# A tensor product pass over sorted edges: its dense part takes 468 destinations instead of 136

## The chip, the cores and the metric

The kernel is one program on one core of a Trainium2 chip. Its inputs lie in the chip's memory, and the metric is the device time in microseconds of one launch. The core's engines are TensorE (PE in the profile, its weight loads apart as PEld), VectorE (DVE), ScalarE (ACT), GpSimd (POOL) and SyncE (SP), which here only issues transfers.

## The reference

Four graph layers run one after the other on 6,250 nodes of 128 channels and 200,000 edges; `dst` is sorted and strongly skewed (node 0 has thousands of edges, node 6,000 about sixteen). The change touches the second layer alone, a tensor product that is linear in the source node's channels `x1` and in the nine numbers `x2` of each edge:

```
for k, (i1, i2, io) in enumerate(_INSTR):
    seg = einsum('uvw,ijk,eui,evj->ewk', weights[k], W3J[k], x1s, x2s) * NORM[k]
    out = out.at[:, e:f].add(seg)
...
agg = segment_sum(out, dst)
```

So a destination's result is the sum over nine components c of a fixed 128x128 matrix `w_mix[c]` times the sum over its edges of x2[c] times h[src], where h are the normalised node features.

## The kernel before

The program is a row of stages with a barrier between them. The stage here is `tensor_pass`, from about 1007 to 2711 us of the span. It has two parts that share the engines.

**The gathered part.** Edges are taken in groups of 1,024 (8 tiles of 128), four groups (u = 0 to 3) to a round. For each group GpSimd gathers the 1,024 rows of h by source with 8 indirect transfers (L3007), into one of four buffers, which it may overwrite once the same u of the round before is summed. VectorE makes one-hots of the destinations in a range of 16 and multiplies them by the nine edge numbers (`hoty`, L3092). TensorE does the group in four slots q = 0 to 3, each with two tiles: `sums` (L3217, 4 instructions of 144 columns; every f32 matmul is two instructions in the trace), then a share of `mix` for the group before (L3232, 18 instructions of 128 columns over a group), in slot 1 also `place_sums` (L3244), and last what the plan of the dense part puts into the slot. ScalarE copies each slot's sums out of PSUM (`take_parts`, L3039) and, at a group's end, the mixed result (`take_mixed`, L3049), for which TensorE's first `mix` of the next group waits, since both use the bank `pm`. VectorE adds the placed result to the accumulator (L3111).

**The dense part** serves the first destinations, those with the most edges, without gathering (class `Dense`). Each destination has a fixed number of visits, each a matmul of 128 edges: a one-hot of the source's low 7 bits against nine edge numbers spread over 49 blocks (L3255, 441 columns), so that a destination's visits sum its weights over all source nodes. After a destination's last visit ScalarE copies the 441 columns into `d_sums` (L3023). After a batch of destinations 49 matmuls multiply h by `d_sums` (`apply_batch`, L3264), ScalarE copies (L3029), nine matmuls mix (`mix_batch`, L3272), and VectorE adds (`add_nodes`). SyncE loads the edges of each destination (L2950, L2951), `prepare` turns them into numbers and masks, and `hots_of_nodes` makes the one-hots for TensorE, a group ahead. `Dense.plan` lays all pieces over the slots. The edges of the first SKIP rounds belong wholly to dense destinations, and the gathered part leaves those rounds out.

SyncE also issues the gathered part's index loads (L2962), each behind the dense loads that stand ahead of it in the program.

Of the kernel before, what the change touches and what calls it, by code (L numbers as in the profile page):

```python
# [27 lines left out]
P = 128  # L28
# [1139 lines left out]
class Dense:  # L1168


    NODES, BATCH, SKIP = 136, 17, 7
    RUN, RING, SLICES, FIRST, TAIL = 2, 6, 7, 32, 12

    def __init__(self, nc, ctx, sh):
# [6 lines left out]
        for b in range(self.batches):  # L1181
            mine = range(b * self.BATCH, (b + 1) * self.BATCH)
            if sum(self.caps[i] for i in mine) % self.RUN:
                self.caps[next(i for i in mine if not i or self.caps[i] < self.caps[i - 1])] += 1
# [5 lines left out]
        assert self.NODES <= 2 * P and self.NODES % self.BATCH == 0 and self.RUN == 2  # L1190
# [8 lines left out]
        self.windows = sb("dense_windows", [1, 1], I32)  # L1199
        self.plan()  # L1200
# [7 lines left out]
    def size(self, b):  # L1208
        return self.first[(b + 1) * self.BATCH] - self.first[b * self.BATCH]

    def room(self):

        return self.size(0) + self.size(1)

    def place_of(self, v):

        b = next(b for b in range(self.batches) if v < self.columns(b).stop)
        return v - self.columns(b).start + b % 2 * self.size(0)

    def places(self, b):  # L1220
        at = self.place_of(self.columns(b).start)
        return slice(at, at + self.size(b))

    def plan(self):


        pieces, gaps = [], 0
        for b in range(self.batches):
            for i in range(b * self.BATCH, (b + 1) * self.BATCH):
                for v in range(self.first[i], self.first[i + 1]):  # L1230
                    pieces.append(("visit", i, v))
            pieces.append(None)
            for k in range(self.SLICES):
                pieces.append(("apply", b, k))
            pieces.append(None)
            pieces.append(("mix", b, 0))
            pieces += [None, None]
# [4 lines left out]
        assert len(pieces) <= room  # L1242
        self.at = [[] for _ in range(slots)]
        for n, piece in enumerate(pieces):
            if piece is not None:
                self.at[self.FIRST + n * room // len(pieces)].append(piece)
        self.hots_at = [[] for _ in range(self.groups)]
        self.prep_at = [[] for _ in range(self.groups)]
        self.adds_at = [[] for _ in range(self.groups)]
        for slot, here in enumerate(self.at):  # L1250
            for kind, n, k in here:
                group = slot // self.parts
                if kind == "visit" and k % self.RUN == 0:
                    self.hots_at[group - 1].append(k)
                    for b in range(self.batches):
                        if k <= self.columns(b).start < k + self.RUN:
                            self.prep_at[group - 2].append(b)
                if kind == "mix":
                    self.adds_at[group].append(n)
        self.loads_at = [[] for _ in range(self.groups)]  # L1260
        for b in range(self.batches):
            after = 0
            if b >= 2:
                after = 4 + next(g for g, here in enumerate(self.hots_at) if self.columns(b - 2).stop - self.RUN in here)
            for n in range(self.BATCH):
                while len(self.loads_at[after]) == 6:
                    after += 1
                self.loads_at[after].append(b * self.BATCH + n)

    def done_before(self, slot):  # L1270

        return self.at[slot - 1] if slot else []


def dense_stage(nc, core, dense):
# [3 lines left out]
    with ExitStack() as ctx:  # L1279
# [16 lines left out]
        p_row = ctx.enter_context(nc.psum_tensor("p_row_dense", [P, 512], F32))  # L1296
        p_all = ctx.enter_context(nc.psum_tensor("p_all_dense", [P, 512], F32))
# [13 lines left out]
        def _(pe):  # L1311
            for c in range(2):
# [3 lines left out]
            nc.tensor.matmul(p_all[:, 0:N + 2], ones[0:1, 0:P], row[:, :], start=True, stop=True).then_inc(row_spread, 1)  # L1316
# [1501 lines left out]
def tensor_pass(nc, core, dense, w_mix, src, src_tiles, attr, attr_laid, table):  # L2818
# [5 lines left out]
    with ExitStack() as ctx:  # L2824
# [13 lines left out]
        PAIRS = J // 2  # L2838
        tiles = U * J
        assert R % 2 == 0  # L2840
        V, B, N, RUN, RING = dense.visits, dense.BATCH, dense.NODES, dense.RUN, dense.RING
        seen, skipped_tiles = dense.seen_tiles, dense.SKIP * U * J
        A = sh.blocks
        wide = Y * A
        assert wide <= 512 and Y * B <= 512
# [12 lines left out]
        moved = sb("moved", [P, 6])  # L2858
# [7 lines left out]
        edge_no = sb("edge_no", [P, seen])  # L2866
        done_far = sb("done_far", [P, seen])
        d_src = sb("d_src", [P, dense.room()], I32)
        d_part = sb("d_part", [P, dense.room()], I32)
        d_lo = sb("d_lo", [P, dense.room()])  # L2870
        d_hi = sb("d_hi", [P, dense.room()])
        d_attr = sb("d_attr", [P, dense.room(), Y])
        d_mask = sb("d_mask", [P, dense.room()])
        d_steps = sb("d_steps", [P, dense.most + 1])
        d_hot = sb("d_hot", [P, RING, P])
        d_row = sb("d_row", [P, RING, Y, A])
        d_sums = sb("d_sums", [P, A, Y, B])
        d_agg = sb("d_agg", [P, Y * B])
        ps = [bank(f"ps{i}") for i in range(4)]
        pm = bank("pm")  # L2880
        p_hot = bank("p_hot")
        hot = p_hot[:, 0:2 * J * RANGE].rearrange("p (s j d) -> p s j d", s=2, d=RANGE)
        steps = p_hot[:, 256:256 + P]
        d_high = p_hot[:, 384:384 + RUN * A].rearrange("p (v a) -> p v a", a=A)
        pw = bank("pw")[:, 0:WIN]
        pd = bank("pd")
# [11 lines left out]
        part_taken = sems("part_taken", 4)  # L2898
# [1801 lines left out]
```

## Time and profile before

| what | value |
|---|---|
| time, median of 3 runs (lowest to highest) | 7041.6 us (7026.89 to 7049.93) |
| span of the profiled execution | 5516.4 us |
| the profiled execution's own time | not among the times; median less span is 1525.2 us |
| busy over the whole span: PE, DVE, ACT, POOL | 76%, 51%, 42%, 69% |
| tensor pass: first gather to the last add | 1015.4 to 2708.3 us |

The span is from the first to the last instruction of the trace; what lies around it has no row. The shares over the whole span are means over stages with different limits, so the rows below are taken from the pass alone.

### The profile page before, as it was taken

How to read it: one execution, taken by the hardware profiler on the slowest of the kernel's cores; microseconds unless marked ns; L12 is line 12 of the kernel's file. 1: busy time of each engine (PE TensorE's matmuls, PEld its weight loads, DVE VectorE, ACT ScalarE, POOL GpSimd, SP SyncE). 2: the span in 40 equal slices, each digit the busy share in tenths (PEclk: the TensorE clock that was granted, in tenths of full speed). 3: DMA queues.
4: the chain of work that ended last, by engine and by line, in shares of the span. 5: the costliest groups of instructions: out<-in, count | busy, mean ns of one | idle time of the engine just before them, and what ended most of it. 6: DMA issues, size and time to landing. Idle time of an engine off the chain costs nothing. (4 is left out here: it accounts for less than half of the span.)

```text
span 5516.4 us, 98683 instructions
## 1 busy us (share of the span) xinstructions
PE 4206.6 (76%) x27638; PEld 3117.4 (57%) x27833; DVE 2829.6 (51%) x8882; ACT 2333.7 (42%) x5698; POOL 3823.3 (69%) x3904
## 2 busy tenths in 40 slices
PE   3399997477777787777757777778777878579985
PEld 2167665355656666656645555555555555446664
DVE  7898665444444444344365555555555555542225
ACT  2545554222222222222366666666666666331003
POOL 0267776677777777777467777777777777477774
PEclk7599998699999999999878888888888888689997
DMA  1134444222222222222233333333333333165552
GB/s 59 43 134 152 165 155 140 69 58 57 59 58 58 60 58 59 58 59 57 53 76 86 78 86 78 82 82 78 86 78 86 78 85 80 40 215 179 173 173 61
DMA packets 357101, 495.36 MB, mean 90 GB/s; under 512 B 198005, under 2 KB 256838, under 8 KB 345798
## 3 DMA queue, kind: packets, MB, share of 16 engines
q0 software_dynamic: 122368, 254.08, 18.2%
q1 hardware_dynamic: 232046, 237.13, 13.9%
q8 instruction: 150, 2.46, 0.2%
q14 instruction: 137, 1.12, 0.1%
q10 hardware_dynamic: 2400, 0.57, 0.1%
HBM read 400.97 MB, written 90.25 MB: 89 GB/s over the span
## 5 line engine op out<-in xcount | busy, mean ns | idle before, releaser
L3482 POOL DMA_INDIRECT rows_l<-table,idx_l x1568 | 1486.4, 948 | 511.0 <-issue 477.2
L3007 POOL DMA_INDIRECT rows_l<-table,idx_l x1344 | 1270.8, 946 | 432.0 <-issue 409.3
L1645 POOL DMA_INDIRECT rows_l<-table,row_idx x896 | 949.3, 1060 | 301.9 <-issue 271.8
L3039 ACT COPY agg_l<-ps_l 128x288 f32<-128x288 f32 x672 | 268.4, 399 | 1266.3 <-PE ps_l L3217 1252.8
L3217 PE MATMUL ps_l<-hoty_l,rows_l 128*128 128x144 f32 x2688 | 511.3, 315 | 350.9 <-DMA rows_l<-table,idx_l 242.7
L3217 PEld LDWEIGHTS ps_l<-hoty_l,rows_l 128*128 128x128 f32 x2688 | 399.1, 199 | 609.5 <-DMA rows_l<-table,idx_l 394.0
L3702 PE MATMUL p_idle_l<-zeros_l 128*128 128x512 bf16 x1373 | 491.8, 520 | 28.0 <-issue 22.3
L3767 PEld LDWEIGHTS banks_l<-wrow_l,hot_l 128*128 128x128 f32 x3136 | 426.6, 200 | 136.2 <-issue 73.0
L3833 ACT ACTIVATE apart_l<-iota,rel_s_l 128x128 bf16<-128x128 f32 x1568 | 497.2, 387 | 10.1
L3767 PE MATMUL banks_l<-wrow_l,hot_l 128*128 128x136 f32 x3136 | 453.4, 289 | 61.0 <-ACT hot_l L3853 61.0
L3232 PE MATMUL pm_l<-w_mix,agg_l 128*128 128x128 f32 x3024 | 468.7, 285 | 0.4 <-ACT msg_l L3049 0.4
L1900 PE MATMUL pa_l<-pieces_l,x_nodes 128*128 128x384 bf16 x2254 | 429.3, 328 | 2.2 <-ACT x_nodes L1694 1.2
L3232 PEld LDWEIGHTS pm_l<-w_mix,agg_l 128*128 128x128 f32 x3024 | 421.7, 201 | 1.0 <-ACT msg_l L3049 0.7
L3111 DVE TENSOR_TENSOR acc<-acc,pw_l 128x128 f32 x168 | 48.4, 288 | 704.2 <-PE pw_l L3244 698.2
L1900 PE MATMUL pa_l<-pieces_l,h_nodes 128*128 128x384 bf16 x2156 | 408.0, 328 | 1.7 <-ACT h_nodes L1694 0.6
L3255 PE MATMUL pd_l<-d_row_l,d_hot_l 128*128 128x441 f32 x744 | 351.8, 555 | 72.1 <-ACT d_sums_l L3023 72.0
L3092 DVE TENSOR_TENSOR hoty_l<-p_hot_l,y_l 128x1152 f32<-128x1152 f32 x168 | 228.1, 1357 | 270.6 <-PE ps_l L3217 268.1
L3702 PEld LDWEIGHTS p_idle_l<-zeros_l 128*128 128x128 bf16 x1568 | 201.8, 129 | 268.8 <-issue 198.5
L1886 PE MATMUL pc_l<-hot_key_l,hot_lo_l 128*128 128x392 bf16 (+1 forms) x1152 | 273.5, 304 | 74.7 <-DVE hot_key_l L1763 70.2
L1900 PEld LDWEIGHTS pa_l<-pieces_l,x_nodes 128*128 128x128 bf16 x2254 | 219.5, 98 | 137.6 <-ACT x_nodes L1694 7.7
L1763 DVE TENSOR_SCALAR hot_key_l<-key_iota_l,key_l 128x392 bf16<-128x392 f16 (+1 forms) x1152 | 293.6, 307 | 0.1
L3530 DVE TENSOR_TENSOR score_l<-rows_l,score_l 128x32 f32<-128x32 f32 x196 | 42.7, 218 | 481.2 <-DMA rows_l<-table,idx_l 481.1
(607 smaller groups left out, 7581.6 us busy)
## 6 DMA issues: line engine op xcount, KB each, us to landing
eT_l<-in_edges_laid SPq DMA_DIRECT2D x196, 256.0 KB
rows_l<-table,idx_l POOLq DMA_INDIRECT x2912
counts_table<-x_nodes SPq DMA_DIRECT2D x22, 1568.0 KB
x_nodes<-counts_table SPq DMA_DIRECT2D x22, 1568.0 KB
counts_table<-h_nodes SPq DMA_DIRECT2D x21, 1568.0 KB
h_nodes<-counts_table SPq DMA_DIRECT2D x21, 1568.0 KB
rows_l<-table,row_idx POOLq DMA_INDIRECT x896
table<-h_nodes SPq DMA_DIRECT2D x21, 448.0 KB
```

Source lines behind the costliest of these rows:

```text
L1645: pool.indirect_dma_start(out=rows[:, slot, j, :], out_offset=None, in_=table, in_offset=bass.IndirectOffsetOnAxis(ap=what[:, j:j + 1], ax ...
L1763: nc.vector.tensor_scalar(hot_key[:, f % RING, 0:near_keys], key_iota[:, 0:near_keys], key[:, t:t + 1], None, ALU.is_equal).then_inc(tile_ ...
L1886: nc.tensor.matmul(pc[m % BANKS][:, at:at + near_keys], hot_lo[:, f % RING, :], hot_key[:, f % RING, 0:near_keys], start=(k % per == 0), s ...
L1900: last = nc.tensor.matmul(pa[n % 2][:, 0:PIECES * D], counts[n % BUFFERS][:, a, :], pieces[:, a, :, :].rearrange("p k d -> p (k d)"), star ...
L3007: pool.indirect_dma_start(out=rows[:, u, j, :], out_offset=None, in_=table, in_offset=bass.IndirectOffsetOnAxis(ap=idx[:, u, j:j + 1], axi ...
L3217: last = nc.tensor.matmul(ps[q][:, at:at + Y * RANGE], rows[:, u, 2 * q + i, :], hoty[:, s, 2 * q + i, :, :].rearrange("p c d -> p (c d)") ...
L3232: last = nc.tensor.matmul(pm[:, 0:D], agg[:, s, c, :, :].rearrange("p t d -> p (t d)"), w_mix[:, c, :], start=(c == 0), stop=(c == Y - 1))
L3255: nc.tensor.matmul(pd[:, 0:wide], d_hot[:, v % RING, :], d_row[:, v % RING, :, :].rearrange("p c a -> p (c a)"), start=(v == dense.first[i ...
L3482: pool.indirect_dma_start(out=rows[:, u, j, :], out_offset=None, in_=table, in_offset=bass.IndirectOffsetOnAxis(ap=idx[:, u, j:j + 1], axi ...
L3702: nc.tensor.matmul(p_idle[:, :], zeros[:, 0:P], zeros[:, :], start=True, stop=True)
L3767: last = nc.tensor.matmul(p_sum[:, 0:WROW], hot[:, s, j, :], wrow[:, s, j, :], start=(j == 0), stop=(j == J - 1))
L3833: last = nc.scalar.activation(apart[:, j, :], core.iota[:, :], ACT.Abs, scale=-1.0, bias=rel_s[:, g.s, j:j + 1])
```

## The change

The dense part takes 468 destinations in 39 batches of 12 (before 136 in 8 batches of 17), and the gathered part skips 13 rounds instead of 7, so it has 144 groups instead of 168. Visits go from 372 to 781, applied blocks from 8 x 49 to 39 x 49 (of 108 columns, before 153). One-hots are made in runs of up to four visits (197 runs, before 186 of two), in a ring of three runs. The dense part's results go into two PSUM banks in turn (`pds`), for which the gathered part's sums share three banks instead of four. `d_sums` is laid so that ScalarE writes the 441 numbers of a destination in one run, and `apply_batch` reads its 108 columns 49 numbers (196 bytes) apart. ScalarE takes a dense result in the same slot in which it is finished, not in the next. The mix of a batch comes two visits into the next batch, and ScalarE copies its result before VectorE adds it. Masks are made for destinations of equal size at once. Pieces are laid over the slots by weights.

```diff
-    NODES, BATCH, SKIP = 136, 17, 7
-    RUN, RING, SLICES, FIRST, TAIL = 2, 6, 7, 32, 12
+    NODES, BATCH, SKIP = 468, 12, 13
+    RUN, RING, SLICES, FIRST, TAIL, LOADS = 4, 3, 7, 20, 8, 7
+    LOADED = 4
...
+                if b and i == next(j for j in mine if self.first[j] >= self.columns(b).start + 2):
+                    uses.append(("mix", b - 1))
+                    pieces.append((("mix", b - 1, 0), 2))
+                uses.append(("visit", i))
                 for v in range(self.first[i], self.first[i + 1]):
-                    pieces.append(("visit", i, v))
+                    pieces.append((("visit", i, v), 5 if v == self.first[i + 1] - 1 else 3))
...
-        d_sums = sb("d_sums", [P, A, Y, B])
+        d_sums = sb("d_sums", [P, B, Y, A])
...
-        ps = [bank(f"ps{i}") for i in range(4)]
+        ps = [bank(f"ps{i}") for i in range(PARTS_HELD)]
...
-        pd = bank("pd")
+        pds = [bank(f"pd{i}") for i in range(2)]
...
+                if i % B == 0:
+                    if b >= LOADED:
+                        wait_loaded(sp, w, b - LOADED)
+                        sp.sem_inc(batch_begun, 1)
+                    if dense.before[b] is not None:
+                        sp.wait_ge(dense_hot, START + w * RUNS + dense.runs_through[dense.before[b]])
...
-                for kind, n, k in dense.done_before(slot):
+                for kind, n, k in dense.at[slot]:
...
-                        nc.scalar.copy(d_sums[:, :, :, n % B].rearrange("p a c -> p c a"),
-                                       pd[:, 0:wide].rearrange("p (c a) -> p c a", a=A)).then_inc(node_taken, 1)
+                        nc.scalar.copy(d_sums[:, n % B, :, :].rearrange("p c a -> p (c a)"), pds[m % 2][:, 0:wide]).then_inc(use_taken, 1)
...
                 if v == dense.first[i]:
-                    if i:
-                        pe.wait_ge(node_taken, START + w * N + i)
+                    pe.wait_ge(use_taken, START + w * USES + max(m - 1, 0))
...
-                    last = nc.tensor.matmul(pd[:, 0:Y * B], core.h[:, a, :], d_sums[:, a, :, :].rearrange("p c i -> p (c i)"),
+                    last = nc.tensor.matmul(pds[m % 2][:, 0:Y * B], core.h[:, a, :], d_sums[:, :, :, a].rearrange("p i c -> p (i c)"),
```

On TensorE, in the middle of the pass, a group before (the numbered names are banks, L3217 sums, L3232 mix, L3244 placing, L3255 a visit):

```order
L3217 MATMUL ps0_l1<-hoty_l1,rows_l1 128x144 x2
L3232 MATMUL pm_l1<-w_mix,agg_l1 128x128 x3
L3217 MATMUL ps1_l1<-hoty_l1,rows_l1 128x144 x2
L3232 MATMUL pm_l1<-w_mix,agg_l1 128x128 x2
L3244 MATMUL pw_l1<-hot_place_l1,msg_l1 128x128
L3255 MATMUL pd_l1<-d_row_l1,d_hot_l1 128x441
L3217 MATMUL ps2_l1<-hoty_l1,rows_l1 128x144 x2
L3232 MATMUL pm_l1<-w_mix,agg_l1 128x128 x2
L3254 REGISTER_ALU
L3255 MATMUL pd_l1<-d_row_l1,d_hot_l1 128x441
```

and after (L3284 sums, L3298 mix, L3310 placing, L3320 a visit):

```order
L3284 MATMUL ps1_l1<-hoty_l1,rows_l1 128x144 x2
L3298 MATMUL pm_l1<-w_mix,agg_l1 128x128 x2
L3310 MATMUL pw_l1<-hot_place_l1,msg_l1 128x128
L3320 MATMUL pd0_l1<-d_row_l1,d_hot_l1 128x441
L3317 REGISTER_ALU
L3320 MATMUL pd1_l1<-d_row_l1,d_hot_l1 128x441
L3281 REGISTER_ALU
L3284 MATMUL ps2_l1<-hoty_l1,rows_l1 128x144 x2
L3298 MATMUL pm_l1<-w_mix,agg_l1 128x128 x2
L3320 MATMUL pd1_l1<-d_row_l1,d_hot_l1 128x441
```

Where a slot held at most one visit, these hold two, in the banks `pd0` and `pd1` in turn, and the sums go round three banks.

On ScalarE, before, in the middle of the pass (L3039 takes sums, L3023 a destination's counts, L3049 the mixed result):

```order
L3039 COPY agg_l1<-ps1_l1 128x9x32
L3036 REGISTER_ALU
L3039 COPY agg_l1<-ps2_l1 128x9x32
L3020 REGISTER_ALU
L3023 COPY d_sums_l1<-pd_l1 128x9x49
L3039 COPY agg_l1<-ps3_l1 128x9x32
L3047 REGISTER_ALU
L3049 COPY msg_l1<-pm_l1 128x128
```

and after (L3099, L3078 and L3109 are the same three):

```order
L3099 COPY agg_l1<-ps2_l1 128x9x32
L3075 REGISTER_ALU
L3078 COPY d_sums_l1<-pd1_l1 128x441
L3098 REGISTER_ALU
L3099 COPY agg_l1<-ps0_l1 128x9x32
L3109 COPY msg_l1<-pm_l1 128x128
```

The copy of a destination's counts has become one run of 441 numbers and stands right behind the sums of its own slot, in slot 3 ahead of the mixed result.

On VectorE, one run of one-hots before:

```order
L3135 TENSOR_TENSOR p_hot_l<-p_hot_l,d_hi_l 128x98
L3137 TENSOR_TENSOR d_hot_l<-p_hot_l,d_lo_l 128x256
L3139 REGISTER_ALU
L3140 TENSOR_TENSOR d_row_l<-p_hot_l,d_attr_l 128x882
```

and after, two runs:

```order
L3201 TENSOR_TENSOR p_hot_l<-p_hot_l,d_hi_l 128x196
L3203 TENSOR_TENSOR d_hot_l<-p_hot_l,d_lo_l 128x512
L3205 REGISTER_ALU
L3206 TENSOR_TENSOR d_row_l<-p_hot_l,d_attr_l 128x1764
L3199 REGISTER_ALU
L3201 TENSOR_TENSOR p_hot_l<-p_hot_l,d_hi_l 128x196
L3203 TENSOR_TENSOR d_hot_l<-p_hot_l,d_lo_l 128x512
L3205 REGISTER_ALU
L3206 TENSOR_TENSOR d_row_l<-p_hot_l,d_attr_l 128x1764
```

A run has the same three operations with twice the elements.

## Rows read from the trace of the kernel before

**Rows 1.** Page, its first line: the span of the profiled execution.
```profile
span 5516.4 us, 98683 instructions
```

**Rows 2.** Windows, tensor pass: busy us by engine, (x) instructions, granted clock, DMA.
```profile
1015.00:2695.00 1680.00, 1284.40 (x7680) 1010.46 (x7681) 684.52 (x1414) 422.21 (x980) 1270.28 (x1344) 0.96 0.24 59
```

**Rows 3.** Groups by line in the tensor pass, 1015 to 2700 us.
```profile
L3007 POOL DMA_INDIRECT rows_l<-table,idx_l x1344 | 1270.8, 946 | 432.0 <-issue 409.3 <-DMA idx_l<-in_src_tiles 22.6
L3217 PE MATMUL ps_l<-hoty_l,rows_l 128*128 128x144 f32 x2685 | 510.6, 315 | 350.9 <-DMA rows_l<-table,idx_l 242.7 <-DVE hoty_l L3092 84.6 <-issue 22.4
L3232 PE MATMUL pm_l<-w_mix,agg_l 128*128 128x128 f32 x3002 | 463.5, 284 | 0.0
L3255 PE MATMUL pd_l<-d_row_l,d_hot_l 128*128 128x441 f32 x744 | 351.8, 555 | 72.1 <-ACT d_sums_l L3023 72.0
L3039 ACT COPY agg_l<-ps_l 128x288 f32<-128x288 f32 x671 | 268.0, 399 | 1263.6 <-PE ps_l L3217 1250.1 <-issue 13.5
L3023 ACT COPY d_sums_l<-pd_l 128x441 f32<-128x441 f32 x136 | 131.0, 963 | 0.0
L3049 ACT COPY msg_l<-pm_l 128x128 f32<-128x128 f32 x166 | 47.1, 284 | 8.9 <-PE pm_l L3232 4.0
```

**Rows 4.** Line L3007: ns min/median/max, first and last start us.
```profile
L3007 POOL DMA_INDIRECT rows_l<-table,idx_l x1344: 940/944/1689, 1015.4 to 2694.6; - x192
```

**Rows 5.** Timeline of TensorE, 2653 to 2661 us: start, length, instructions.
```profile
2653.30 0.39 PE L3244 MATMUL pw_l<-hot_place_l,msg_l 128*128 128x128 f32 x2
2653.52 1.99 PE L3264 MATMUL pd_l<-d_sums_l,h_nodes 128*128 128x153 f32 x14
2655.35 0.65 PE L3217 MATMUL ps_l<-hoty_l,rows_l 128*128 128x144 f32 x4
2655.84 0.61 PE L3232 MATMUL pm_l<-w_mix,agg_l 128*128 128x128 f32 x4
...
2657.83 0.61 PE L3232 MATMUL pm_l<-w_mix,agg_l 128*128 128x128 f32 x4
2658.27 2.08 PE L3272 MATMUL pd_l<-d_agg_l,w_mix 128*128 128x17 f32 x18
2660.20 0.74 PE L3217 MATMUL ps_l<-hoty_l,rows_l 128*128 128x144 f32 x4
```

**Rows 6.** Lines L3255 and L3264: ns min/median/max of one instruction.
```profile
L3255 PE MATMUL pd_l<-d_row_l,d_hot_l x744: 533/536/947, 1101.3 to 2626.2; 128*128 128x441 f32 x186
...
L3264 PE MATMUL pd_l<-d_sums_l,h_nodes x784: 291/293/462, 1459.3 to 2655.2; 128*128 128x153 f32 x196
```

**Rows 7.** Windows of two other stretches: sum pass, and the pass's end.
```profile
400.00:500.00 100.00, 99.73 (x723) 72.17 (x722) 92.80 (x295) 51.19 (x112) 79.27 (x69) 1.00 0.41 144
...
2680.00:2690.00 10.00, 7.84 (x39) 7.19 (x40) 0.49 (x2) 1.86 (x5) 7.56 (x9) 0.66 0.21 54
```

**Rows 8.** Groups by line of VectorE in the tensor pass.
```profile
L3092 DVE TENSOR_TENSOR hoty_l<-p_hot_l,y_l 128x1152 f32<-128x1152 f32 x168 | 228.1, 1357 | 270.6 <-PE ps_l L3217 268.1 <-DVE p_hot_l L3080 1.3 <-issue 0.2
L3135 DVE TENSOR_TENSOR p_hot_l<-p_hot_l,d_hi_l 128x98 f32<-128x98 f32 x186 | 48.9, 263 | 6.5 <-PE pd_l L3255 0.2
L3137 DVE TENSOR_TENSOR d_hot_l<-p_hot_l,d_lo_l 128x256 f32<-128x256 f32 x186 | 77.1, 414 | 0.3
L3140 DVE TENSOR_TENSOR d_row_l<-p_hot_l,d_attr_l 128x882 f32<-128x882 f32 x186 | 198.2, 1066 | 0.0
```

**Rows 9.** Timeline of SyncE's queue, two loads one after the other.
```profile
1470.42 0.33 SPq L2950 DMA_DIRECT2D d_src_l<-in_src  x1
...
1472.02 0.59 SPq L2950 DMA_DIRECT2D d_src_l<-in_src  x1
```

**Rows 10.** Lines L567 and L569, order stage: ns min/median/max.
```profile
L567 PE MATMUL pl_order<-rel,down_order x2: 532/614/697, 30.1 to 30.6; 128*128 128x196 f32 x2
...
L569 PE MATMUL pr_order<-joined_order,up_order x2: 534/615/696, 34.4 to 34.9; 128*128 128x196 f32 x2
```

**Rows 11.** Timeline, the last add of the tensor pass.
```profile
2707.99 0.29 DVE L3111 TENSOR_TENSOR acc<-acc,pw_l 128x128 f32 x1 [0.74 <-PE pw_l L3244]
```

More of the change, by code:

```diff
@@ L1208, in size, with lay_columns @@
     def size(self, b):
-        return self.first[(b + 1) * self.BATCH] - self.first[b * self.BATCH]
-    def room(self):
-        return self.size(0) + self.size(1)
+        return self.columns(b).stop - self.columns(b).start
+    def lay_columns(self):
+        self.room = self.size(0) + self.size(1)
+        self.begin, self.before, at = [], [], 0
+        for b in range(self.batches):
+            if at + self.size(b) > self.room:
+                at = 0
+            over = [c for c in range(b) if self.begin[c] < at + self.size(b) and at < self.begin[c] + self.size(c)]
+            self.begin.append(at)
+            self.before.append(max(over) if over else None)
+            at += self.size(b)
@@ L1249, in plan @@
         self.adds_at = [[] for _ in range(self.groups)]
+        made_at, begun_at = {}, {}
+        starts = {v: r for r, (v, _) in enumerate(self.runs)}
         for slot, here in enumerate(self.at):
@@ L1315, in _ @@
             pe.wait_ge(row_ready, START + 1)
-            nc.tensor.matmul(p_all[:, 0:N + 2], ones[0:1, 0:P], row[:, :], start=True, stop=True).then_inc(row_spread, 1)
+            for at in range(0, N + 2, 512):
+                end = min(at + 512, N + 2)
+                last = nc.tensor.matmul(p_all[:, at:end], ones[0:1, 0:P], row[0:1, at:end], start=True, stop=True)
+            last.then_inc(row_spread, 1)
         @block.vector
@@ L2844, in tensor_pass @@
         wide = Y * A
-        assert wide <= 512 and Y * B <= 512
+        marks = range(0, seen, P)
+        kinds = sorted(set(dense.caps))
+        assert wide <= 512 and Y * B <= 512 and J * RANGE + P + RUN * A <= 512
         rel = sb("rel", [P, G, J])
@@ L2921, in tensor_pass @@
         shares = ((0, 3), (3, 5), (5, 7), (7, 9))
-        prep_count = 4 * dense.batches + N + dense.batches
+        prep_count = 2 * dense.batches
+        loads_of = [2 * B * DMA * len(range(i, dense.batches, LOADED)) for i in range(LOADED)]
         def count_windows(engine):
@@ L2989, in _ @@
                 sp.wait_ge(idx_loaded[u], START + windows * (R * DMA))
-            for b in range(dense.batches):
-                sp.wait_ge(dense_loaded[b], START + windows * (2 * B * DMA))
+            for i in range(LOADED):
+                sp.wait_ge(dense_loaded[i], START + windows * loads_of[i])
             for i in range(2):
@@ L3269, in mix_batch @@
             def mix_batch(w, b):
[L3270 removed]
+                m = dense.use_of["mix", b]
+                pe.wait_ge(use_taken, START + w * USES + max(m - 1, dense.use_of["apply", b] + 1))
                 for c in range(Y):
[L3272 removed]
+                    last = nc.tensor.matmul(pds[m % 2][:, 0:B], w_mix[:, c, :], d_agg[:, :, c], start=(c == 0), stop=(c == Y - 1))
                 last.then_inc(batch_mixed, 1)
```

254 lines of the change are left out of this document (144 added, 110 removed).

## The prediction

> **What bounds the kernel now.** I read the page for the span [rows 1], then the windows of the stage that changes, then its groups by line, and only then single instructions. In the pass TensorE is busy 1284 of 1680 us, GpSimd 1270, VectorE 685 and ScalarE 422 [rows 2]. No share decides by itself, so I read what ended the idle time. GpSimd's 1344 gathers wait for "issue" alone, but for the first one [rows 3], and start every (2694.6 - 1015.4) / 1343 = 1.250 us [rows 4]: it never waits for a buffer. TensorE's sums sat idle 351 us, 243 of them for gathered rows [rows 3]. So the pass goes at GpSimd's pace, 8 x 1.25 = 10.0 us a group, and lasts from 1015.4 to the last add, 2708.3 [rows 4, 11]: 1693 us. Fewer groups shorten it only as long as TensorE needs under 10.0 us a group with what it is given in their place.
>
> **What TensorE needs.** Busy time overlaps and holds waits, so I price by the distance between starts where nothing waits. Four instructions of sums take 2655.84 - 2655.35 = 0.49 us, four of mix 0.44, placing 0.22 [rows 5]. A group has 16, 18 and 2 of them: 1.96 + 1.98 + 0.22 = 4.16 us. For columns, the medians 536 ns at 441 and 293 ns at 153 [rows 6] give 243 / 288 = 0.844 ns a column; what is left over is the drain, which the next instruction covers. A visit is then 2 x 441 x 0.844 = 0.744 us. The 14 applied instructions took 1.83 us, 0.131 each, as the slope says for 153 columns. But 18 instructions of only 17 columns took 1.93 us [rows 5], 0.107 each: below about 127 columns the weight load sets the pace. The 108 columns of the new apply fall under that.
>
> Before: 168 x 4.16 = 699, visits 277, apply 103, mix 15, together 1094 us under 1680 of GpSimd. After:
> - gathered part, 144 x 4.16: 599
> - 781 visits x 0.744: 581
> - apply, 39 x 49 x 2 = 3822 x 0.107: 409
> - mix, 39 x 9 x 2 = 702 x 0.107: 75
>
> That is 1664 us, 11.6 a group, while GpSimd needs 144 x 10.0 = 1440. The 24 groups give back 240 us on GpSimd and 100 on TensorE, and TensorE takes on 304 + 306 + 60 = 670. **The bound moves to TensorE**, and most of GpSimd's gain is lost to it.
>
> The clock of TensorE matters, since it is now all TensorE. The pass had 0.96 on the mean [rows 2]. It was 1.00 of full speed (2.4 GHz) in a stretch with TensorE 99.7% busy, and 0.66 at the end of the pass with TensorE busy 78% even at the slower pace [rows 7]. I take 1.00, where the 1664 us stand; at 0.96 they would be 69 more.
>
> **The sum.** The plan leaves the first 20 slots, five groups, without dense work, so these run at GpSimd's pace: TensorE has group 5's first rows after 42 gathers, 52.5 us, plus about 2 for their way (chosen between nothing and the 13.7 us from last gather to last add [rows 4, 11]). From there 1664 - 5 x 4.16 = 1643 us of work. Behind it some 4 us of mix, placing and adds.
>
> Waits on top. ScalarE now takes a destination's counts in the same slot. In 81 of 144 groups slot 3 ends with a destination's last visit, and the first mix of the next group needs the mixed result that ScalarE copies only after those counts. The scattered copy took 963 ns; the copies of 288 and 128 numbers took 399 and 284 [rows 3], 0.72 ns a number, so 441 in one run should take 509. That is 0.2 (drain) + 0.5 + 0.3 (mixed result, part overlapped) against 0.49 of sums: about 0.5 us each, 41 us. If the copy stayed at 963 it is 0.45 more each, 77; if ScalarE starts earlier than I think, nothing. The 72 us that visits waited for that copy [rows 3] go, hidden by the second bank, but they were no part of the bound. The apply comes a slot after the last visit, whose sums and mix (0.93) cover the copy.
>
> VectorE: by the slopes of its four operations [rows 8] a run of four visits costs 0.36 + 0.66 + 2.02 = 3.0 us, 197 of them 598; 144 groups at 1.36 + three small ones of 0.29 are 320, the preparation some 70. Near 990 us beside 1740 is hidden, but a group with three runs has 11.3 of 11.6 us; I put 10 us for such places.
>
> SyncE: a destination's two loads and register load take 1.60 us [rows 9]. 468 are 749 us, seven in a group 11.2; index loads queue behind them and behind the new wait for `dense_hot`. GpSimd has 1.6 us a group to spare and a lead of up to four groups, so this is nothing; without that cover each late index load would add what it is late.
>
> The setup (rows of 468 numbers on one partition, one more PSUM bank, nine small mask tables) is a few operations longer: 5 us, chosen, between nothing and 10.
>
> Pass: 55 + 1643 + 4 + 41 + 10 = 1753 against 1693, +60; with the setup +65. The profiled span would go from 5516 to about 5581. The profiled execution's own time isn't recorded; the median is 1525 us above the span [rows 1], and I let that stand: **7107 us**, +0.9%.
>
> **A rule against the change.** `apply_batch` now reads each number 196 bytes from the last. The nearest row is a matmul whose moving operand lies 32 bytes apart, L567: 614 ns, against 615 for L569 with the same 196 columns side by side [rows 10]. By these it costs nothing; both ran early, at a slow clock, so full speed isn't shown. The Trainium skill, "SBUF — State Buffer", section "Door 1: The DMA port swizzle", says that SBUF delivers lines of 16 bytes and that each access which crosses to a new line pays a penalty, so that f32 may stride over 4 numbers for free. It gives no size.
>
> **Rivals.**
> 1. *The strided read halves the streaming rate.* 108 columns would cost 108 x 2 x 0.844 = 0.182 us instead of 0.107, times 3822: +287, to 7394. The trace has no such stride at full clock, which speaks for leaving it open; rows 10 speak against. 0.08.
> 2. *TensorE is the bound but waits for almost nothing* (ScalarE early, VectorE ahead): 55 + 1643 + 4 + 5 = 1707 against 1693, 7056: no change by the measure below. 0.15.
> 3. *The chains around it are late*: VectorE in groups with two or three runs, behind ring and placing; ScalarE's copy at 963; SyncE's index loads behind `dense_hot`. One us in each of 70 such groups and 36 more for the copy give 7200; twice the first 7270. 0.12.
> 4. *Faster.* If a second visit that follows at once in a slot costs only half, 0.37, its 323 cases save 120 us: 6987. It decides from 83 us saved, 0.26 a case. For it: no two visits stand back to back in the old trace. Against: all f32 instructions that follow one another keep the 0.844 a column, 14 in a row too. With it I count the case that GpSimd stays the bound (7041.6 - 240 = 6802), which needs 1.6 us a group out of prices read from rows. 0.08.
>
> The forecast's own case has 0.57.
>
> **Numbers.** About 0.3%, 21 us, is what a measurement of this kernel can tell from no change. Faster (below 7020): rival 4, 0.08. Same (7020 to 7063): rival 2 and the near edge of the forecast, 0.17. Slower: the rest, 0.75. The range runs from just under rival 2 to the middle of rival 3, 7045 to 7230; outside are rivals 1 and 4 and the far end of 3, about 0.2.
>
> **What will show it.** Right: GpSimd waits for sums (`summed`) instead of issue alone; gathers 12 us a group on the mean; TensorE over 90% busy from group 5 on, granted clock near 1.00; apply instructions 0.107 apart; contiguous copy near 0.51; 0.5 us gaps before the first mix of a group, released by ScalarE's `msg`. Wrong: gathers still every 1.25 us; apply at 0.18; sums or visits released by VectorE; a clock that stays at 0.96 or falls although TensorE is full; or a changed difference between time and span.

## The result

The changed kernel took **7350.7 us** (median of 4, 7341.2 to 7376.6) against 7034.3 us for the kernel before (median of 4, 7024.5 to 7049.9): a ratio of **1.0461, 95% interval 1.0434 to 1.0487**. The forecast was 7107 us with a range of 7045 to 7230: the kernel is slower as forecast, but by five times as much, and outside the range.

The profile after, its first line, the window of the pass from first to last gather (its columns: stretch, length, busy us of PE, PEld, DVE, ACT and POOL, granted clock, DMA share, GB/s), and its groups by line (the same views as rows 1, 2 and 3):

```profile
span 7346.6 us, 109114 instructions
```

```profile
1151.00:3596.00 2445.00, 2106.19 (x11012) 1753.48 (x11012) 879.61 (x1441) 480.18 (x1242) 1090.03 (x1152) 0.93 0.17 36
```

```profile
L3061 POOL DMA_INDIRECT rows_l<-table,idx_l x1152 | 1091.0, 947 | 1377.1 <-issue 929.7 <-PE ps_l L3284 377.3 <-DMA idx_l<-in_src_tiles 59.2
L3331 PE MATMUL pd_l<-d_sums_l,h_nodes 128*128 128x108 f32 x3724 | 754.8, 375 | 69.9 <-ACT d_sums_l L3078 54.6 <-issue 14.7
...
L3320 PE MATMUL pd_l<-d_row_l,d_hot_l 128*128 128x441 f32 x1558 | 699.2, 564 | 145.5 <-ACT d_sums_l L3078 110.1 <-issue 34.1 <-DVE d_row_l L3206 1.2
L3298 PE MATMUL pm_l<-w_mix,agg_l 128*128 128x128 f32 x2516 | 403.2, 290 | 77.7 <-ACT msg_l L3109 44.0 <-issue 33.2
L3284 PE MATMUL ps_l<-hoty_l,rows_l 128*128 128x144 f32 x2252 | 397.9, 302 | 68.7 <-issue 51.4 <-ACT agg_l L3099 16.1 <-DMA rows_l<-table,idx_l 1.2
...
L3078 ACT COPY d_sums_l<-pd_l 128x441 f32<-128x441 f32 x465 | 245.2, 530 | 622.7 <-PE pd_l L3320 315.1 <-remote 232.3 <-issue 75.3
```

Three things are to be seen. The span is 7346.6 us and this execution's own time 7348.4: nothing lies outside the span, so the kernel before, which takes 7034, can't be the execution of 5516 us that the first profile showed. The apply (L3331) keeps TensorE busy for 755 us, where I gave it 409, and each instruction lasts longer (375 ns for 108 columns) than one of 153 columns did [rows 6]. And TensorE is idle for 339 us while it waits for ScalarE and for "issue", although it has the most work.

### The profile page after: what moved, and what is told of

It is laid out like the page before. It is cut to its first block and busy times, and to the rows that moved or that the text cites. A ratio compares the mean times of both kernels' runs of the same rounds, so it can differ in the third digit from the quotient of the medians.

```text
span 7346.6 us, 109114 instructions
## 1 busy us (share of the span) xinstructions
PE 5468.0 (74%) x31192; PEld 4161.8 (57%) x31387; DVE 3015.7 (41%) x8930; ACT 2403.7 (33%) x5980; POOL 3627.9 (49%) x3712
## 5 line engine op out<-in xcount | busy, mean ns | idle before, releaser
L3550 POOL DMA_INDIRECT rows_l<-table,idx_l x1568 | 1483.8, 946 | 1269.4 <-issue 1012.0
L3061 POOL DMA_INDIRECT rows_l<-table,idx_l x1152 | 1091.0, 947 | 1377.1 <-issue 929.7
L3835 PE MATMUL banks_l<-wrow_l,hot_l 128*128 128x136 f32 x3136 | 716.3, 398 | 501.1 <-DVE wrow_l L3732 286.1
L3835 PEld LDWEIGHTS banks_l<-wrow_l,hot_l 128*128 128x128 f32 x3136 | 650.3, 296 | 687.6 <-issue 502.1
L3331 PE MATMUL pd_l<-d_sums_l,h_nodes 128*128 128x108 f32 x3822 | 774.5, 375 | 69.9 <-ACT d_sums_l L3078 54.6
L3320 PE MATMUL pd_l<-d_row_l,d_hot_l 128*128 128x441 f32 x1562 | 701.2, 564 | 148.0 <-ACT d_sums_l L3078 111.4
L3331 PEld LDWEIGHTS pd_l<-d_sums_l,h_nodes 128*128 128x128 f32 x3822 | 736.4, 219 | 81.5 <-ACT d_sums_l L3078 57.1
L3099 ACT COPY agg_l<-ps_l 128x288 f32<-128x288 f32 x576 | 232.0, 405 | 1008.9 <-PE ps_l L3284 477.8
L3284 PEld LDWEIGHTS ps_l<-hoty_l,rows_l 128*128 128x128 f32 x2304 | 384.0, 204 | 238.8 <-issue 213.2
L3589 DVE TENSOR_REDUCE score_l<-bank_s_l 128x32 f32<-128x128 f32 x196 | 57.4, 293 | 1105.8 <-remote 1099.7
L3298 PE MATMUL pm_l<-w_mix,agg_l 128*128 128x128 f32 x2592 | 414.8, 290 | 78.4 <-ACT msg_l L3109 44.7
L3284 PE MATMUL ps_l<-hoty_l,rows_l 128*128 128x144 f32 x2304 | 406.6, 302 | 68.7 <-issue 51.4
L3078 ACT COPY d_sums_l<-pd_l 128x441 f32<-128x441 f32 x468 | 246.7, 530 | 623.0 <-PE pd_l L3320 315.5
L3320 PEld LDWEIGHTS pd_l<-d_row_l,d_hot_l 128*128 128x128 f32 x1562 | 274.2, 200 | 297.3 <-issue 195.4
```

The costliest lines, as they stand in the source:

```text
L3061: pool.indirect_dma_start(out=rows[:, u, j, :], out_offset=None, in_=table, in_offset=bass.IndirectOffsetOnAxis(ap=idx[:, u, j:j + 1], axi ...
L3284: last = nc.tensor.matmul(bank_of(g, q)[:, at:at + Y * RANGE], rows[:, u, 2 * q + i, :], hoty[:, s, 2 * q + i, :, :].rearrange("p c d -> p ...
L3298: last = nc.tensor.matmul(pm[:, 0:D], agg[:, s, c, :, :].rearrange("p t d -> p (t d)"), w_mix[:, c, :], start=(c == 0), stop=(c == Y - 1))
L3320: nc.tensor.matmul(pds[m % 2][:, 0:wide], d_hot[:, r % RING, place, :], d_row[:, r % RING, place, :, :].rearrange("p c a -> p (c a)"), sta ...
L3331: last = nc.tensor.matmul(pds[m % 2][:, 0:Y * B], core.h[:, a, :], d_sums[:, :, :, a].rearrange("p i c -> p (i c)"), start=(a == 0), stop= ...
L3550: pool.indirect_dma_start(out=rows[:, u, j, :], out_offset=None, in_=table, in_offset=bass.IndirectOffsetOnAxis(ap=idx[:, u, j:j + 1], axi ...
```

## The experiments

The runs fall into two kinds. Beside the result and in experiments 1 to 3 the kernel before took 6975 to 7034 us, in all runs of experiment 4 it took about 5510. A ratio is always to the kernel before, run beside the others on the same chip. A pass is given from its first to its last gather unless said otherwise.

**1. What was profiled, and what was timed.** The two kernels again, unchanged.

> The kernel before, unchanged, profiled again: its first profile spans 5516 us while its timed runs take 7025 to 7050, and the changed kernel's profile spans 7347 beside a time of 7348. Theory A (the first profile stands for the timed runs and some 1500 us lie outside the span): span near 5516 again, gathers of the attention stage every 1.25 us. Theory B (the first profile caught an execution unlike the timed ones): span near 7030, attention stage longer by about 750 us, and the tensor pass near what the changed kernel's trace less 316 us leaves.

> The changed kernel, unchanged, profiled again beside the kernel before on the same chip. Theory A and B both: span near 7347. If its apply instructions again stand about 0.2 us apart where the kernel before has 0.13, the strided read is the first suspect; if everything on TensorE is longer alike, the clock is.

Before: 6975.0 us with a span of 6973.2. After: 7254.6 with 7252.8. So theory B holds. The pass of the kernel before, window and groups by line:

```profile
1124.00:3265.00 2141.00, 1438.51 (x7575) 1201.54 (x7575) 676.37 (x1401) 398.58 (x963) 1269.82 (x1344) 0.80 0.19 46
```

```profile
L3007 POOL DMA_INDIRECT rows_l<-table,idx_l x1344 | 1270.7, 945 | 893.6 <-issue 721.2 <-PE ps_l L3217 62.9 <-DMA x_nodes<-in_x 55.9
L3232 PE MATMUL pm_l<-w_mix,agg_l 128*128 128x128 f32 x2944 | 552.4, 324 | 334.2 <-ACT msg_l L3049 200.3 <-issue 133.6
L3217 PE MATMUL ps_l<-hoty_l,rows_l 128*128 128x144 f32 x2633 | 522.1, 327 | 95.3 <-issue 82.6 <-DVE hoty_l L3092 10.5 <-DMA rows_l<-table,idx_l 1.8
L3255 PE MATMUL pd_l<-d_row_l,d_hot_l 128*128 128x441 f32 x744 | 429.9, 665 | 269.0 <-ACT d_sums_l L3023 183.1 <-issue 77.9 <-DVE d_row_l L3140 4.0
```

It takes 2141 us where [rows 4] had 1679. The gathers of a group still start 1.25 us apart, but behind the eighth GpSimd pauses (3.43 us to the next start at the median). TensorE waits for gathered rows for 1.8 us instead of 243 [rows 3], and for ScalarE instead. The place to look is a wait whose releaser had been free, here in the timeline (start, length, engine; some lines left out):

```profile
1864.96 0.91 PE L3255 MATMUL pd_l<-d_row_l,d_hot_l 128*128 128x441 f32 x2
...
1865.39 0.94 POOL L3007 DMA_INDIRECT rows_l<-table,idx_l  x1 [0.30 <-issue]
...
1866.19 0.61 PE L3232 MATMUL pm_l<-w_mix,agg_l 128*128 128x128 f32 x4
...
1866.64 0.94 POOL L3007 DMA_INDIRECT rows_l<-table,idx_l  x1 [0.30 <-issue]
...
1869.56 0.97 ACT L3023 COPY d_sums_l<-pd_l 128x441 f32<-128x441 f32 x1
1870.01 0.94 POOL L3007 DMA_INDIRECT rows_l<-table,idx_l  x1 [2.43 <-DMA x_nodes<-in_x]
...
1870.66 1.83 PE L3255 MATMUL pd_l<-d_row_l,d_hot_l 128*128 128x441 f32 x2 [3.86 <-ACT d_sums_l L3023]
```

The visit ends at 1865.87, and the copy that waits for it starts 3.7 us later, though ScalarE stood idle from 1866.7 to 1869.3 and then did one copy of 0.40 us. The next visit waits 3.86 us for that copy. What the copy waited for is TensorE's semaphore. The trace holds the time at which a semaphore was increased, and the visit's came at 1869.18 us, 3.31 us after the visit's end; those of the sums and of a mix, which ended by 1866.8, came at 1869.24 and 1869.30. I compared these times with the modelled end of the matmul that makes the increase, by where that end lies in GpSimd's train of gathers, that is the eight gathers of a group (kernel before, 1200 to 3200 us; the median is of the lateness, late is over 0.4 us):

```
end of the matmul, us after the train's start   late   median, us
0 to 0.5                                           3%      0.01
1.5 to 2.5                                        29%      0.01
4 to 6                                            64%      1.95
6 to 8                                            94%      3.84
8 to 10                                           98%      2.55
```

Late ones come up in bunches. Of those in the last two rows, 60% come 2.3 to 3.2 us after the start of the train's last gather, that is about 1.7 us after its end. In the same pass of the first profile 4 of 1259 were late.

The shares are upper bounds. This trace holds 36,904 increases in all, the first profile 99,274, and where one is missing the next one is taken, which then looks late. Counted only where no second matmul with the same semaphore had ended in between, 569 of 1043 are late in the kernel before and 459 of 1282 in the changed kernel's first profile. Counted the same way, the increases of ScalarE, VectorE and GpSimd are on time in all but 7 of 1527 cases (kernel before); whether the missing ones were late isn't known. These rows gave theory G: while GpSimd runs a train of gathers, TensorE's semaphores come up late.

**2. The stride, the copy, the amount of dense work.** The apply's read made side by side, in one kernel by reading other numbers (the output isn't the reference's), in the other by the layout of before; 42 of 49 applied blocks left out; and the new code with the old numbers. Of each edit the main lines:

```diff
# a1_flat, g_flat
-                    last = nc.tensor.matmul(pds[m % 2][:, 0:Y * B], core.h[:, a, :], d_sums[:, :, :, a].rearrange("p i c -> p (i c)"),
+                    last = nc.tensor.matmul(pds[m % 2][:, 0:Y * B], core.h[:, a, :], d_sums[:, :, :, :].rearrange("p i c a -> p (i c a)")[:, a * (Y * B):(a + 1) * (Y * B)],
# a1_contig, g_contig
-        d_sums = sb("d_sums", [P, B, Y, A])
+        d_sums = sb("d_sums", [P, A, Y, B])
...
# a2_seventh
-                for a in range(first, end):
+                for a in range(k, k + 1):
...
# a3_136
-    NODES, BATCH, SKIP = 468, 12, 13
-    RUN, RING, SLICES, FIRST, TAIL, LOADS = 4, 3, 7, 20, 8, 7
+    NODES, BATCH, SKIP = 136, 17, 7
+    RUN, RING, SLICES, FIRST, TAIL, LOADS = 2, 3, 7, 20, 8, 7
```

> The changed kernel, in which the apply reads the same 108 numbers' worth of d_sums side by side instead of 196 bytes apart (they are then the wrong numbers, so the output isn't the reference's; work, waits and copies stay the same). Theory S, the strided read slows the stream: in the changed kernel's second profile the 3736 applied instructions take 755 us of TensorE, 0.202 each, where all other kinds stand 1.2 to 1.4 times above my prices. Side by side they should take 0.107 x 1.3 = 0.14, which saves 0.06 x 3822 = 230 us of a pass that TensorE bounds: a time of 7120, 150 to 360 us under the changed kernel. Theory W, TensorE is slowed as a whole (lower clock, late semaphores) and the stride costs nothing: within 30 us of the changed kernel's 7350.

> The changed kernel with d_sums laid as before: the apply reads side by side, and ScalarE's copy scatters again (963 ns instead of 530). The output is the reference's. Theory S: the gain of the side-by-side read (150 to 360 us) less what the slower copy costs. If that copy lies on the path in 81 groups, 0.45 us each, it gives back 36 us; if in every one of 468 destinations, 200 us. Theory W: 0 to 200 us slower than the changed kernel.

> The changed kernel with 7 of the 49 applied blocks of each batch (42 left out, 3276 of 3822 instructions, so the output isn't the reference's). It prices the apply where it stands. If TensorE's work is the bound, 3276 x 0.202 = 660 us go, until GpSimd's pace holds it: 144 groups at the 12.74 us that a group took in the kernel before's second profile are 1835 us of pass, 570 less than now: time near 6780. If the pass is held by the chains around TensorE (ScalarE's copies, late semaphores), the gain is under 300 us: above 7050.

> The changed kernel's code with the numbers of the kernel before: 136 destinations, batches of 17, 7 rounds skipped, runs of two in a ring of three runs. It parts the new mechanisms (two banks, contiguous copy, strided apply, three banks for the sums, copy in the same slot, weights) from the amount of dense work. Theory D, the amount of dense work makes the loss: within 40 us of the kernel before (784 applied instructions at 0.06 more are 47 us of TensorE, which isn't the bound there). Theory M, the mechanisms lose by themselves: 60 us or more slower than before.

| kernel | median us | ratio (95%) | pass, first to last gather |
|---|---|---|---|
| a1_flat | 7260.0 | 1.0321 (1.0264 to 1.0377) | 2368 |
| a1_contig | 7276.7 | 1.0347 (1.0291 to 1.0404) | 2376 |
| a2_seventh | 6978.0 | 0.9932 (0.9908 to 0.9956) | 2091 |
| a3_136 | 7029.9 | 1.0009 (0.9979 to 1.0038) | 2143 |

The amount of dense work makes the loss: with the old numbers of destinations, batches and rounds the new code costs nothing, within 0.4%. The read side by side takes the apply's distance from start to start from 193 to 112 ns, 310 us of TensorE's work, yet the ratio falls only from 1.046 to 1.032. Theory S was right that the read costs, but expected 150 to 360 us, and about 98 came out (0.014 of 7020; by the two intervals roughly 50 to 140). Of the 632 us (3276 x 0.193) that a2_seventh takes away, 5.3% or 370 us come out, less than the first reading expected (570) and more than the second (under 300). There GpSimd also sat idle for 253 us until an index load had landed (34 times; 59 us and 6 times in the changed kernel's first profile), so that SyncE's loads, a piece of rival 3, may hold part of the rest. In both kernels the granted clock of TensorE over the pass is lower, 0.90 in a1_flat and 0.87 in a2_seventh after 0.93: it stood at 1.2 GHz instead of 2.4 for longer. The slower copy costs 17 us in the medians, inside the intervals.

**3. Theory G.** Plain transfers for gathers in this pass, and gathers released in pairs.

```diff
# d_before_plain, d_after_plain
-                            pool.indirect_dma_start(
-                                out=rows[:, u, j, :], out_offset=None, in_=table,
-                                in_offset=bass.IndirectOffsetOnAxis(ap=idx[:, u, j:j + 1], axis=0),
-                            ).then_inc(rows_loaded[u][j // 2], DMA)
+                            pool.dma_start(rows[:, u, j, :], table[j * P:(j + 1) * P, :]).then_inc(rows_loaded[u][j // 2], DMA)
# f_after_pairs, f_before_pairs, f_contig_pairs, g_before_pairs; from the second round on
-                        pool.wait_ge(summed[u], START + t)
-                        pool.sem_inc(group_begun, 1)
-                        for j in range(J):
+                        for q in range(PAIRS):
+                            if q < PAIRS - 1:
+                                pool.wait_ge(part_summed, t * (U * (PAIRS - 1)) + (START + (u - U) * (PAIRS - 1) + q + 1))
+                            else:
+                                pool.wait_ge(summed[u], START + t)
+                            pool.sem_inc(group_begun, 1)
+                            for j in (2 * q, 2 * q + 1):
...
```

`part_summed` counts the slots that TensorE has summed, and `PAIRS` is 4.

> The kernel before, in whose tensor pass alone GpSimd starts 8 plain transfers of the same size a group instead of 8 gathers (it always brings the first 1024 rows, so the output isn't the reference's). Theory G: while GpSimd runs a train of gathers, the semaphores of TensorE's matmuls come up late. In the kernel before's second profile, of the matmuls with a semaphore that ended 6 to 10 us into a train over nine in ten were told over 0.4 us late, most of them about 2.7 us after the start of the train's last gather, and of those that ended outside a train almost none. TensorE then waits for engines that wait for it, and the pass takes 2141 us though its work at full clock is 1094. Without gathers the pass should fall to 1100 to 1450 us, the time to 6000 to 6330. Theory L: the lateness is TensorE's own (clock, queue), the gathers have nothing to do with it: TensorE stays at 12 to 12.7 us a group, the time falls by under 150 us.

> The changed kernel with the same edit: plain transfers instead of gathers in the tensor pass (output not the reference's). Theory G: what is left is TensorE's own work: 144 x 4.16 + 781 x 0.744 + 702 x 0.107 + 3822 x 0.193 (the start-to-start distance of its strided apply) = 1993 us at full clock, plus short waits: a pass of 2000 to 2150 instead of 2445, a time of 6900 to 7060. The loss of the change would then be far larger than with gathers, since before falls by more. Theory L: within 80 us of the changed kernel's 7350.

> The changed kernel with the same gathers, but from the second round on GpSimd waits before each pair of gathers for the sums of that pair four groups earlier, instead of once a group for all eight. The trains of eight should break into pairs with pauses. Theory G: TensorE's semaphores are then held for 2 to 4 us instead of up to 8, TensorE's 340 us of idle time shrink, and the clock rises: 80 to 200 us under the changed kernel's 7350. If the pauses are shorter than the 1.7 us after a gather's end at which held semaphores come up, nothing changes. Theory L: no change (within 30 us).

> The kernel before with the same edit, gathers released in pairs. Its TensorE is idle for 700 of the pass's 2141 us in its second profile. Theory G: 50 to 400 us faster than the kernel before; with pauses under 1.7 us nothing, or slower if GpSimd's 10 us of issuing a group no longer fit between the releases. Theory L: no change, or slower for the same reason.

| kernel | median us | ratio (95%) | pass | semaphores late |
|---|---|---|---|---|
| d_before_plain | 6067.5 | 0.8693 (0.8674 to 0.8712) | 1242 | 0 of 1243 |
| d_after_plain | 6874.3 | 0.9844 (0.9820 to 0.9869) | 2027 | 0 of 1505 |
| f_after_pairs | 7113.0 | 1.0200 (1.0175 to 1.0226) | 2253 | 611 of 1506 |
| f_before_pairs | 6913.7 | 0.9891 (0.9857 to 0.9925) | 2062 | 668 of 1128 |

Without gathers in the pass not one semaphore there is late, and both passes fall to what theory G gave (the changed kernel's time, 6874, is 26 us under its 6900 to 7060); the attention stage behind, whose gathers stayed, takes 2682 and 2688 us (first to last gather) as it does with them (2686 in the kernel before's second profile). The cleaner of the two is d_after_plain, since there GpSimd's pace isn't the bound: its pass, first to last transfer, has TensorE busy for 98% at a granted clock of 0.99, and with 2027 us nearly that of the changed kernel in the other kind of run, with its gathers (2051 us, g_after below).

```profile
1128.00:3155.00 2027.00, 1986.70 (x10988) 1687.32 (x10989) 878.06 (x1437) 493.59 (x1238) 608.86 (x1151) 0.99 0.19 44
```

In d_before_plain GpSimd's 10.0 us a group go too, so its 1242 us lie below the 1679 of the first profile, and not all of its 13% is lateness. What in a gather does the holding isn't parted by these runs: the plain transfers need no index, always read the same 1,024 rows, and start 0.53 us apart at the median instead of 1.25.

Pairs take the changed kernel from 1.046 to 1.020, some 180 us, and the kernel before down by 1.1%: f_before_pairs beats both kernels. That they help through fewer late semaphores isn't shown. In the kernel before 59% are late with pairs and 61% without, in the changed one 41% and 50%; the earlier release of GpSimd alone could do it. The window of d_before_plain, set against that of the kernel before in experiment 1, shows TensorE at 0.98 instead of 0.80 of its full clock, with the same work of its own:

```profile
1139.00:2381.00 1242.00, 1129.93 (x7570) 968.86 (x7571) 675.68 (x1404) 410.14 (x965) 710.43 (x1343) 0.98 0.31 80
```

**4. Both mends, and the other kind of run.** The side-by-side read with plain transfers, and the layout of before with pairs (their edits are those shown above, put together); then four kernels again.

> The changed kernel with plain transfers instead of gathers in the tensor pass and, as in the run with the side-by-side read, the apply's 108 numbers read side by side (output not the reference's twice over). With gathers that read saved only 78 to 90 us of time. Theory G: it was worth the full 3822 x (0.193 - 0.112) = 310 us of TensorE's work, and late semaphores and the lower clock ate the rest; where TensorE is the whole bound the 310 come out: 6874 - 310 = 6565, a pass near 1720. Theory E (something else ends the pass): under 150 us less than 6874.

> The changed kernel with both mends, output as the reference: d_sums laid so that the apply reads side by side, and gathers released in pairs. The pairs took the changed kernel from 1.046 to 1.020 times the kernel before, the layout to 1.035. If they add up: 1.009, 7090 to 7100 on a chip where before takes 7034, or 7045 where it takes 6981. If the layout's 310 us come out more fully because fewer semaphores are late: 0.98 to 1.00. If TensorE waits more as its work shrinks, as with the layout alone: 1.01 to 1.02.

They took 5590.3 us, ratio 1.0145 (1.0127 to 1.0163), and 5657.1, ratio 1.0268 (1.0250 to 1.0287), beside a kernel before of 5509.9. The expected times don't apply, and 1.0268 is outside all three ratios that I gave for the second. But the pass of d_after_flat_plain is 1722 us where 1720 was expected, 305 less than d_after_plain's 2027, both with no late semaphore and at a granted clock of 0.99: there the read is worth nearly its full 310 us. The time of the kernel before beside them is that of my first profile, and f_contig_pairs, with all its gathers, has 4 late semaphores of 1528: these two belong to the other kind of run. So the changed kernel itself had to be measured there.

> The changed kernel as it is. On a chip where before takes about 5510: TensorE's work with the strided read is 1993 us; with the 55 of GpSimd's start, 41 of waits for the mixed result, 4 and 10 the pass is 2103 against 1693, so 5510 + 410 + 5 = 5925, 1.075 times before. On a chip where before takes about 7000: 1.04 to 1.05 as measured twice.

> The changed kernel with the apply's 108 numbers read side by side (the wrong ones, so output not the reference's). On a chip of 5510: 3822 x 0.081 = 310 us under g_after, 5615, which is my forecast's pass of 1753 with its prices. On a chip of 7000: 70 to 100 us under g_after.

> The changed kernel with d_sums laid as before, output as the reference. On a chip of 5510: the slower copy (979 ns instead of 530) adds its 0.45 us in the 81 groups in which it stands before the mixed result, 36 us over g_flat: 5650, as the same kernel with gathers in pairs took (5657). On a chip of 7000: within 20 us of g_flat.

> The kernel before with gathers released in pairs. On a chip of 5510 GpSimd waits for nothing, so more releases can only add their own issue time (3 more waits a group, 164 groups): between 0 and 30 us slower. On a chip of 7000: 0.985 to 0.99 of before, as measured.

| kernel | median us | ratio (95%) |
|---|---|---|
| g_after, the changed kernel | 5917.9 | 1.0728 (1.0710 to 1.0746) |
| g_flat | 5610.6 | 1.0171 (1.0154 to 1.0188) |
| g_contig | 5655.2 | 1.0258 (1.0241 to 1.0276) |
| g_before_pairs | 5513.4 | 0.9996 (0.9986 to 1.0005) |

The expectations were 5925, 5615, 5650 and 0 to 30 us slower; the last came out 1.5 us faster, inside the noise. The windows of the pass of g_after and of g_flat, from the first gather to the last add, and 28 applied instructions in the timeline of each, with the line that follows:

```profile
1018.00:3109.00 2091.00, 2038.53 (x11270) 1733.59 (x11270) 885.73 (x1453) 503.44 (x1266) 1089.71 (x1152) 0.99 0.20 42
```

```profile
1019.00:2799.00 1780.00, 1726.88 (x11270) 1422.27 (x11270) 885.60 (x1454) 504.18 (x1266) 1092.28 (x1152) 0.99 0.23 50
```

```profile
1500.77 5.57 PE L3331 MATMUL pd_l<-d_sums_l,h_nodes 128*128 128x108 f32 x28
1506.16 0.67 PE L3284 MATMUL ps_l<-hoty_l,rows_l 128*128 128x144 f32 x4
```

```profile
1557.91 3.27 PE L3331 MATMUL pd_l<-d_sums_l,h_nodes 128*128 128x108 f32 x28
1561.02 0.67 PE L3284 MATMUL ps_l<-hoty_l,rows_l 128*128 128x144 f32 x4
```

The first pair of lines is g_after, 5.39 us for 28 (0.193 each), the second g_flat, 3.11 us (0.111 each). TensorE is 97% busy in both windows and at 0.99 of full speed, and between them 311 us of pass are gone: the whole 3822 x 0.081.

## Why the prediction was wrong

**"the median is 1525 us above the span [rows 1], and I let that stand".** This step failed. The 1525 us are no time around the span. In every run since, an execution's own time is about 2 us above its span. The profile was of one kind of execution and the timed runs of the other, in which the stages themselves are longer: this pass 2141 instead of 1679 us, attention 2686 instead of 1963. Every price of mine was read in the one and added to the other. The prediction had named "a changed difference between time and span" as a sign of being wrong; it came.

**"So the pass goes at GpSimd's pace", and "The bound moves to TensorE".** True where few semaphores are late (g_before_pairs still needs 1679 us with more waits on GpSimd). In the timed runs the kernel before needs 12.7 us a group, because GpSimd waits for sums whose semaphore comes late, and TensorE waits for ScalarE, which learns of its matmuls late. I had GpSimd's pace as the cover behind which TensorE's 586 us of spare time could be filled, and the overlap came out otherwise. On one chip the pass went from 2141 to 2402 us: TensorE's busy time rose by 655 (1439 to 2093) and its idle time fell by 393 of 702, to 309. That is +261 where I had +60. Idle time of this kind does take in a little work: in a3_136 the strided read puts 784 x (273 - 130) ns = 112 us more onto TensorE, and the pass stays at 2143.

In the timed runs the change cost 316 us where I had 65. About 100 of them are the strided read. The other 225 or so (a1_flat's ratio) are what the rest of the change costs there; the same kernel costs 96 us in the other kind of run (g_flat). So some 130 us hang on the kind of run. That late semaphores make them is argued from the waits and from d_after_plain, not shown by a run of its own.

**"By these it costs nothing" (the strided read).** This step failed too, and what came is rival 1, which had 0.08. That its 7394 us lie near the measured 7351 is luck: in those runs the read cost about 100 us and not 287. The distance is 193 ns for 108 numbers, 1.79 ns a number; I had 182 in the rival and 107 in the sum. In a3_136 it is 273 ns for 153 numbers, 1.78 each, at either level of the clock, against 130 ns side by side at 2.4 GHz and 254 at 1.2 in the kernel before. The rows that spoke against it [rows 10] are at a slow clock, where little of the penalty is left to see: 273 against 254 ns for 153 numbers, and for 108 none, since they are 213 ns apart with the stride and without it, which is also the distance of instructions of only 12 or 17 columns at that clock. And the stride in those rows was 32 bytes, which no run here has at full clock. I said that full speed wasn't shown, and should have left the price open between both ends. The Trainium skill, "SBUF — State Buffer", section "Door 1: The DMA port swizzle", with its lines of 16 bytes, holds here in direction: 193 ns against 112.

**The rest of the sum**, by g_flat, which has my prices' conditions: pass 1780 us from first gather to last add (the window above), forecast 1753; its ratio of 1.0171 is +96 us, forecast +65. Of the 27 missing, 17 are the apply at 111.5 instead of 107 ns. By g_after's rows the contiguous copy took 527 ns (forecast 509), the wait for the mixed result 28 us (forecast 41), waits for VectorE 35 us in 2 places (forecast 10 in all), the setup 2 us (forecast 5), and the clock stood at 0.99. Had this kind of run been timed, the forecast of +65 us would have met +403 (5917.9 less 5514.9), most of it the stride: 307 us by the times of g_after and g_flat. One sum of the prediction is off without effect: rival 4 would decide from 87 us saved (7107 less 7020), not 83.

**How the stride shrinks to about 100 us with late semaphores.** a1_flat shows where the 310 us went: TensorE's busy time fell by only 197 us against the changed kernel's first profile (2106 to 1909), at a lower clock (0.93 to 0.90), and its idle time rose by 120 (339 to 459). That the waits caused the lower clock is argued from these rows, not shown by itself; d_before_plain, with the work of the kernel before, 112 us idle instead of 702, and 0.98, speaks for it.

**Rivals 2 and 4** didn't come. Rival 3 has the right sign and place (chains around TensorE), but the waits that grew are for ScalarE and "issue", behind late semaphores, and not for VectorE (1.2 us before visits) or a longer copy (530 ns).

## What stays open

What decides which kind of run one gets is not settled. The number of the chip, as recorded, is no answer: experiment 1 and the last four kernels both name a chip 9, in one kind and in the other. Whether that is the same chip isn't known. Nor is it shown what between GpSimd and TensorE holds the semaphores up, and why gathers of the same length hold none in the other kind of run. That it takes the gathers is shown by d_before_plain and d_after_plain.

## What to carry to other kernels

Before adding anything up, hold the profile's span against the timed runs: 5516 against 7034 meant another execution, and the first question is which stage holds the difference. A read whose numbers lie far apart is priced at full clock by its own row or at two prices, never at the price of one at a slow clock. And releasing a group's gathers in smaller parts cost nothing in one kind of run and gained 1.1% (kernel before) in the other.

## What the runs showed of the hardware

- In one kind of run semaphores of TensorE's matmuls came up to 6 us and more after the modelled end while GpSimd ran a train of gathers (over 0.4 us late: 55 to 61% in the kernel before, 36 to 50% in the changed one), and 14 ns after it otherwise. With 8 plain transfers a group, also started by GpSimd, none was late. In the other kind of run, with the same gathers, 4 of 1259 were. The Trainium skill, "Perfetto Trace Analysis", section "Tensor Engine Instruction (MATMUL, LD_WEIGHTS)", says that a matmul's end is estimated and its semaphore is pushed when PSUM has acknowledged the bytes. The 14 ns of the semaphores on time agree with an estimate close to it.
- An f32 moving operand at a stride of 196 bytes streamed at 1.79 ns a number, side by side at 0.84. For 153 numbers that is 273 ns at 2.4 GHz and at 1.2 GHz alike, where side by side it is 130 and 254. For 108 numbers it is 193 and 213 ns, side by side 112 and 213.
